# Graph layers on one core: the edge gathers read 128 table rows each instead of 125

## The chip, the cores and the metric

One Trainium2 chip; the program runs on one of its cores. The metric is the time of the whole program on the device, in microseconds (us), lower being better. The engines are named as the profile names them: PE (TensorE, PEld its weight loads), DVE (VectorE), ACT (ScalarE), POOL (GpSimd) and SP (SyncE). SP issues the plain transfers here, POOL the gathers.

## The reference: what is computed

`x` holds 3125 nodes of 256 features; `src` and `dst` are the ends of 50000 edges, ordered by `dst`. Two graph blocks follow each other, each with attention over the nodes and a mixture of experts beside or behind it. What matters here are three passes over all edges:

```python
# two GATv2 layers (one head), each:
xj = (x @ Wl)[src]
h = leaky_relu(xj + (x @ Wr)[dst] + eattr @ We, 0.2)
logits = h @ att
ex = exp(logits - segment_max(logits, dst)[dst])
out = segment_sum(xj * ex[:, None], dst) / segment_sum(ex, dst)[:, None]
...
# later one attention layer with 8 heads of 32 features:
e = leaky_relu(eh[src] + ee + et[dst], 0.2)
ex = exp(e - segment_max(e, dst)[dst])
rst = segment_sum(ft[src] * ex[:, :, None], dst) / segment_sum(ex, dst)
```

In each pass every edge needs the row of its source node from a table in DRAM: a gather of 50000 rows, of 261, 258 and 272 float32 values (1044, 1032 and 1088 bytes) in the three passes.

## The kernel before

**Tiles.** The 3125 nodes are 25 tiles of 125, the 50000 edges 400 tiles of 125. An edge tile that touches two node tiles is worked once for each, so that a pass has S = 432 steps (some of them padding), in NG = 27 groups of G = 16. One step takes one gather of 125 rows, one row to each partition. `schedule` makes the table of row numbers, `c.src_s`, one column for each step.

**One pass** is the function `messages`; it runs three times (stage names `msg1`, `msg2`, `msg3`; the first two with `one` true, the third with eight heads). The profile shows all three under the same names `msg_rows`, `msg_cur` and so on. All engines walk the same groups, each in an instruction stream of its own with a loop over three groups, and meet at semaphores:

- DVE copies the 16 columns of row numbers of a group to `msg_cur` (L142).
- POOL issues 16 gathers a group at L705, into one of RB = 3 buffers of `msg_rows`. Four gathers are a block with a semaphore of its own (`landed[q][b]`). POOL may only start on a block when the sums that read the buffer's last content are done (`summed`).
- SP loads for each group a broadcast of node numbers (`msg_oht`, 875 KB and 101.6 KB) and the masks `msg_pens`.
- PE, for group j+1, multiplies one-hot rows with the destination table (L912; L922 in the third pass) and adds the gathered rows (L916, only in the first two passes), and waits at steps 0, 4, 8 and 12 of a group for the block to land. Between these it sums group j-1 over its edges (L958). At L929 it transposes the logits of group j, once a group: the starts of L929 count the groups off.
- DVE does max, product and sum for the logits (L750, L758, L759), the running maxima, and adds the sums of PE to the totals (L840). In the third pass it also scales the gathered rows (L821) and reads them for the logits (L767), for which it waits for all four blocks.
- ACT scales the gathered rows in the first two passes (L1021) and makes the one-hot matrices.

Before its first group DVE clears the totals (L873) and, in the first two passes, works out the edge terms (L877, L878).

Of the kernel before, what the change touches and what calls it, by code (L numbers as in the profile page):

```python
# [14 lines left out]
I32 = mybir.dt.int32  # L15
# [4 lines left out]
N, D, E = 3125, 256, 50000  # L20
P = 125
EVEN = 112
NT = N // P
ET = E // P
ER = 100
EB = ET // ER
G = 16
S = 432
NG = S // G
RB = 3  # L30
# [4 lines left out]
U = 5  # L35
CN = NT // U

# [157 lines left out]
def transpose_tiles(nc, name, c, src, dst_t, gcol=None, bcol=None, rep=None):  # L195
# [3 lines left out]
    with Stage(nc, name, rep) as st:  # L199
        pt = [[st.ps(f"pt{j}_{k}", [128, P]) for k in range(bufs)] for j in range(2)]  # L200
        turned = st.sem("turned", NT)
        out = [st.sem(f"out{j}", NT) for j in range(2)]
        with st.block() as block:
            @block.tensor
            def _(pe):
                for t in range(NT):
                    if t >= bufs:

                        for j in range(2):
                            pe.wait_ge(out[j].sem, out[j].at(t - bufs + 1))  # L210
                    for j in range(2):
                        last = nc.tensor.transpose(pt[j][t % bufs], src[:, t, j * 128:(j + 1) * 128], c.ident[0:P, 0:P])
                    last.then_inc(turned.sem, 1)

            @block.scalar
            def _(act):
                for t in range(NT):
                    act.wait_ge(turned.sem, turned.at(t + 1))
# [7 lines left out]
            def _(dve):  # L226
                for t in range(NT):
                    dve.wait_ge(turned.sem, turned.at(t + 1))
# [43 lines left out]
def schedule(nc, c, src, dst, ea2, pick, pen):  # L272
# [3 lines left out]
    with Stage(nc, "sch") as st:  # L276
# [28 lines left out]
        sp_ = [st.ps(f"sp{j}", [P, S]) for j in range(6)]  # L305
# [8 lines left out]
        with st.block() as block:  # L314
# [19 lines left out]
            def _(dve):  # L334
                ch = Chain(dve, order)
# [43 lines left out]
                ch(nc.vector.tensor_copy(c.nt_row[:], ntf[0:1, :]))  # L379

                ch(nc.vector.memset(c.src_s[:], 0))
                ch(nc.vector.tensor_copy(c.src_s[:, 0:S], sp_[1][:]))
                ch(nc.vector.memset(c.rel[:], 0.0))
                ch(nc.vector.memset(c.eas[:], 0.0))
                ch(nc.vector.tensor_copy(dsts[:], sp_[2][:]))
# [227 lines left out]
def messages(nc, name, call, c, table, heads, dst_rows, edge_lin, att, acc, marks, ee):  # L613
# [6 lines left out]
    TW = table.shape[1]  # L620
# [3 lines left out]
    PAIRS = G // 2  # L624
    QS = G // 4
    with Stage(nc, name) as st:
        rows = st.sb("rows", [P, RB, G, TW])
        cur = st.sb("cur", [P, RB, G], I32)
        oh = st.sb("oh", [P, RB, G, P])
        oht = st.sb("oht", [K1, RB, G * P])  # L630
        pens = st.sb("pens", [R, RB, 4, P])
# [61 lines left out]
        with st.block() as block:  # L693
            @block.gpsimd
            def _(pool):
                def gather(g, u, i, first):
                    q = u % RB
                    pool.wait_ge(slot_ready.sem, slot_ready.at(g + 1))
                    pool.sem_inc(issued.sem, 1)
                    for b in range(4):  # L700
                        if not first:
                            pool.wait_ge(summed.sem, summed.at((g - RB) * G + (b + 1) * QS))
                            pool.sem_inc(issued.sem, 1)
                        for k in range(b * QS, (b + 1) * QS):
                            nc.gpsimd.indirect_dma_start(out=rows[:, q, k, :], out_offset=None, in_=table,  # L705
                                                         in_offset=bass.IndirectOffsetOnAxis(ap=cur[:, q, k:k + 1], axis=0)).then_inc(landed[q][b].sem, 16)

                for g in range(RB):
                    gather(g, g, 0, True)
                with pool.Fori(0, NG // RB - 1) as i:  # L710
                    for u in range(RB, 2 * RB):
                        gather(i * RB + u, u, i, False)
# [331 lines left out]
def even_parts(ap):  # L1044


    return [(0, EVEN), (EVEN, P)] if ap.shape[0] == P else [(0, ap.shape[0])]

# [1943 lines left out]
def program(nc, I, out):  # L2992
# [12 lines left out]
    c = Consts()  # L3005
    with Stage(nc, "c") as st:
# [1 line left out]
        c.ones_row, c.blocks, c.part = st.sb("ones_row", [1, 512]), st.sb("blocks", [128, 128]), st.sb("part", [128, 1])  # L3008
        c.lin = st.sb("lin", [P, NT])
        c.iota_low = st.sb("iota_low", [P, 16])  # L3010
        c.nt_row, c.src_s = st.sb("nt_row", [1, S], I32), st.sb("src_s", [P, S + G], I32)
        c.rel, c.last, c.eas = st.sb("rel", [P, S]), st.sb("last", [P, S]), st.sb("eas", [P, S, 2])
        c.link, c.gl, c.gf, c.gb = st.sb("link", [1, S + 1]), st.sb("gl", [1, S + 1]), st.sb("gf", [1, NG, G + 1]), st.sb("gb", [1, NG, G + 1])
        c.pen_d, c.rel_d, c.ea_d = scratch("pen_d", [S, 4 * P]), scratch("rel_d", [NG, G * P]), scratch("ea_d", [2, NG, G * P])
# [20 lines left out]
        with Stage(nc, "mx") as s1:  # L3035
            m = s1.sb("m", [P, NT, D])
            norm_table(nc, "nt", c, I, m, c.lin, xn_d, tabs_d[0], xr_d)
            q = s1.sb("q", [P, NT, D])
# [44 lines left out]
        with Stage(nc, "m0") as s1:  # L3083
            gate = s1.sb("gate", [P, 2, NT])
            src_row, dst_row, expert_row = s1.sb("src_row", [P, tiles0], I32), s1.sb("dst_row", [P, tiles0], I32), s1.sb("expert_row", [1, tiles0], I32)
            rows = s1.sb("mv", [P, NT, 2]), s1.sb("rstd", [P, NT]), s1.sb("off", [P, NT])
# [37 lines left out]
            with Stage(nc, "ma") as s2:  # L3124
# [4 lines left out]
                q, k, v = (s2.sb(n, [P, NT, D]) for n in "qkv")  # L3129
# [17 lines left out]
        with Stage(nc, "m1") as s1:  # L3147
            gate = s1.sb("gate", [P, 1, NT])
            src_row, dst_row, expert_row = s1.sb("src_row", [P, tiles1], I32), s1.sb("dst_row", [P, tiles1], I32), s1.sb("expert_row", [1, tiles1], I32)
            rows = s1.sb("mv", [P, NT, 2]), s1.sb("rstd", [P, NT]), s1.sb("off", [P, NT])  # L3150
# [36 lines left out]
```

## Time and profile before

| | |
|---|---|
| time, median of 3 runs | 5575.98 us (5551.09 to 5578.87) |
| the profiled execution, its own time | 5525.67 us |
| its span, first to last instruction | 5523.5 us |
| granted TensorE clock, mean over the span | 0.838 |
| PE busy | 4451.3 us (81%) |
| DVE busy | 2840.2 us (51%) |
| POOL busy | 1959.6 us (35%), of which the 1296 gathers of the passes 1654.3 us |

The gathers of the passes run from 1737.2 us to 4748.3 us of the span, in three stretches. Shares of the whole span say little about a pass, which has limits of its own; a pass is read from its own stretch: 1737 to about 2430 us, 2660 to about 3355 us, 4034 to about 4770 us. An "idle before" of an engine with "issue" behind it is time in which nothing that the profile shows was waited for.

### The profile page before, as it was taken

The page shows a single profiled execution, that of the slowest core. Times are in us where ns is not written, and L with a number is a line of the kernel's source. Part 1 is how long each engine was busy: PE and PEld are TensorE (multiplying, and loading weights), DVE is VectorE, ACT ScalarE, POOL GpSimd, SP SyncE. Part 2 cuts the span into 40 slices and gives each one's busy share as a digit, 9 for nine tenths or more (in the row PEclk, how much of TensorE's full clock was granted, in tenths as well). Part 3 has the DMA queues.
Part 4 walks back from the last instruction along what each step waited for, and adds up shares of the span by engine and source line. Part 5 has one row for each costly group of instructions (what it writes and reads, how often), then busy time and mean ns, then how long its engine had stood idle before and what let it go on. Part 6 is the DMA issues. An engine that isn't in the chain of part 4 may idle for free. (4 is left out here: it accounts for less than half of the span.)

```text
span 5523.5 us, 80735 instructions
## 1 busy us (share of the span) xinstructions
PE 4451.3 (81%) x21805; PEld 3611.6 (65%) x21806; DVE 2840.2 (51%) x8512; ACT 2155.2 (39%) x6526; POOL 1959.6 (35%) x1535
## 2 busy tenths in 40 slices
PE   4649999999995999997789998479468888655694
PEld 2237978888794777765577775379356666445694
DVE  3127263452722666654466664553646666628424
ACT  0124443434442666652366663313333333221222
POOL 0000000000003778840687882046268777300141
PEclk8879999999997999987899997679665555677697
DMA  3340000000004555530555554442565555210613
GB/s 76 82 137 10 1 17 10 17 9 3 16 15 103 124 128 124 128 87 10 119 124 121 128 122 86 140 133 69 123 147 133 128 125 126 66 44 15 210 36 84
DMA packets 423900, 465.87 MB, mean 84 GB/s; under 512 B 223748, under 2 KB 360950, under 8 KB 423111
## 3 DMA queue, kind: packets, MB, share of 16 engines
q1 hardware_dynamic: 228634, 263.29, 18.9%
q0 software_dynamic: 190976, 197.68, 16.2%
q8 instruction: 114, 1.87, 0.1%
q10 hardware_dynamic: 4000, 1.60, 0.1%
q14 instruction: 176, 1.43, 0.1%
HBM read 398.30 MB, written 62.47 MB: 83 GB/s over the span
## 5 line engine op out<-in xcount | busy, mean ns | idle before, releaser
L705 POOL DMA_INDIRECT msg_rows<-tab_d,msg_cur x1296 | 1654.3, 1276 | 1799.0 <-DVE msg_cur L142 1379.7
L958 PE MATMUL msg_agp<-msg_rows,msg_oh 125*125 125x261 f32 (+2 forms) x2592 | 884.4, 471 | 36.1 <-DVE gv_acc L840 27.0
L958 PEld LDWEIGHTS msg_agp<-msg_rows,msg_oh 125*125 125x125 f32 x2592 | 561.2, 229 | 158.9 <-issue 39.7
L912 PE MATMUL msg_zp<-g_xr,msg_oht 127*125 x1728 | 552.7, 402 | 61.7 <-DVE msg_oht L745 61.3
L916 PE MATMUL msg_zp<-msg_rows,c_ident 125*125 125x256 f32 x1728 | 530.8, 388 | 39.8 <-DMA msg_rows<-tab_d,msg_cur 39.7
L1010 ACT ACTIVATE msg_dist<-c_iota,c_rel 125x125 f32<-125x125 f32 x1296 | 492.8, 386 | 46.5 <-PEq L2983 31.6
L750 DVE SCALAR_TENSOR_TENSOR msg_hid<-msg_zp,g_att 125x256 f32<-125x256 f32 x864 | 360.1, 419 | 279.1 <-PE msg_zp L916 266.7
L1014 ACT ACTIVATE msg_oh<-msg_dist,c_ones 125x125 f32<-125x125 f32 x1296 | 492.7, 386 | 0.0
L1000 ACT ACTIVATE msg_ex<-msg_arg 125x16 f32<-125x16 f32 (+1 forms) x81 | 20.0, 247 | 1019.5 <-DVE msg_delta L814 1019.5
L916 PEld LDWEIGHTS msg_zp<-msg_rows,c_ident 125*125 125x125 f32 x1728 | 331.9, 193 | 100.9 <-DMA msg_rows<-tab_d,msg_cur 46.1
L840 DVE TENSOR_TENSOR gv_acc<-gv_acc,msg_agp 125x261 f32 (+1 forms) x864 | 364.1, 421 | 63.2 <-PE msg_agp L958 54.6
L912 PEld LDWEIGHTS msg_zp<-g_xr,msg_oht 127*125 127x125 f32 x1728 | 310.6, 192 | 116.6 <-issue 62.7
L1281 PE MATMUL mix_pb<-mix_ht,mix_w 128*128 128x125 f32 x3200 | 373.5, 275 | 0.0
L1290 PE MATMUL mix_pc<-mix_w,mix_ut 128*125 128x256 f32 x1600 | 361.8, 380 | 7.1 <-ACT mix_ut L1422 7.1
L1281 PEld LDWEIGHTS mix_pb<-mix_ht,mix_w 128*128 128x128 f32 x3200 | 365.6, 192 | 0.4
L1021 ACT ACTIVATE msg_rows<-msg_rows,msg_ex 125x257 f32<-125x257 f32 x864 | 354.3, 497 | 1.7
L1290 PEld LDWEIGHTS mix_pc<-mix_w,mix_ut 128*125 128x125 f32 x1600 | 292.9, 188 | 47.9 <-issue 8.3
L1557 DVE TENSOR_TENSOR mix_t<-mix_pc,mix_b 125x256 f32<-125x256 f32 x100 | 42.5, 425 | 543.5 <-PE mix_pc L1290 543.5
L1243 PE MATMUL mix_pb<-mix_wp,mix_ht 128*125 128x256 f32 x1200 | 282.7, 387 | 4.1 <-ACT mix_ht L1362 4.1
L840 DVE TENSOR_TENSOR ga_acc<-ga_acc,msg_agp 125x264 f32 x432 | 184.4, 427 | 181.4 <-PE msg_agp L958 157.3
L1243 PEld LDWEIGHTS mix_pb<-mix_wp,mix_ht 128*125 128x125 f32 x1200 | 222.6, 192 | 36.4 <-issue 5.5
L1422 ACT ACTIVATE mix_ut<-mix_pb,mix_b 128x125 f32<-128x125 f32 x800 | 215.4, 391 | 30.9 <-PE mix_pb L1281 30.8
(545 smaller groups left out, 7122.0 us busy)
## 6 DMA issues: line engine op xcount, KB each, us to landing
msg_oht<-rel_d SPq DMA_DIRECT2D x81, 875.0 KB
msg_rows<-tab_d,msg_cur POOLq DMA_INDIRECT x1296, 3.9
ee_raw<-in_edge_attr SPq DMA_DIRECT2D x50, 224.0 KB
msg_pens<-pen_d SPq DMA_DIRECT2D x270, 31.2 KB, 8.0
msg_oht<-rel_d SPq DMA_DIRECT2D x81, 101.6 KB
mix_w<-in_L_mix_W SPq DMA_DIRECT2D x8, 1024.0 KB
m0w_wr<-in_L_ffn_w SPq DMA_DIRECT2D x16, 512.0 KB
m0w_w2r<-in_L_ffn_w SPq DMA_DIRECT2D x16, 512.0 KB
```

Of the source, the lines that this page charges most:

```text
L705: nc.gpsimd.indirect_dma_start(out=rows[:, q, k, :], out_offset=None, in_=table, in_offset=bass.IndirectOffsetOnAxis(ap=cur[:, q, k:k + 1] ...
L750: last = nc.vector.scalar_tensor_tensor(out=hid[:, k, :], in0=zp[:, pair_bank(u, k // 2), (k % 2) * D:(k % 2 + 1) * D], scalar=0.0, in1=at ...
L840: nc.vector.tensor_tensor(a_t, a_t, agp[:, sum_bank(u, k), 0:AW], ALU.add).then_inc(combined.sem, 1)
L912: nc.tensor.matmul(z, hots, d_t, start=True, stop=False)
L916: last = nc.tensor.matmul(z, c.ident[0:P, 0:P], rows[:, u % RB, k, 0:D], start=False, stop=True)
L958: nc.tensor.matmul(agp[:, sum_bank(u, k), 0:AW], oh[:, u % RB, k, :], rows[:, u % RB, k, 0:AW], start=True, stop=True).then_inc(summed.sem, 1)
L1010: nc.scalar.activation(dist[:, k % 4, :], c.iota[0:P, 0:P], ACT.Abs, scale=-1.0, bias=c.rel[:, bass.ds(g * G + k, 1)]).then_inc(dist_ready ...
L1014: last = nc.scalar.activation(oh[:, u % RB, k - 1, :], dist[:, (k - 1) % 4, :], ACT.Relu, scale=-1.0, bias=c.ones[0:P, 0:1])
L1021: nc.scalar.activation(r, r, ACT.Copy, scale=ex[:, u % RB, k:k + 1]).then_inc(scaled.sem, 1)
L1243: last = nc.tensor.matmul(pb[bank][0:P, lo:lo + D], ht[:, t % HR, kc, :], wp[:, w, kc, :], start=(kc == 0), stop=(kc == 1))
L1281: last = nc.tensor.matmul(out, w1[:, kc, f * 128:(f + 1) * 128], ht[:, t % HR, kc, :], start=(kc == 0), stop=(kc == 1))
L1290: last = nc.tensor.matmul(pc[t % 2][0:P, 0:D], ut[:, t % 2, f, :], w2[:, f, :], start=(f == 0), stop=(f == FC - 1))
```

## The change

Each gather of a pass now takes 128 row numbers and fills 128 partitions of `msg_rows`. The three added partitions of the table of row numbers stay zero, so that they fetch row 0; nothing reads them. All other instructions see the first 125 partitions as before, but for the copy to `msg_cur`, which is 128 partitions high. The number of gathers, their order and their waits are the same, and so are the instructions of the other engines. The gathers of the two expert stages (98 there and 98 back) stay at 125 rows.

```diff
+ROWS = 128
...
                 ch(nc.vector.memset(c.src_s[:], 0))
-                ch(nc.vector.tensor_copy(c.src_s[:, 0:S], sp_[1][:]))
+                ch(nc.vector.tensor_copy(c.src_s[0:P, 0:S], sp_[1][:]))
...
-        rows = st.sb("rows", [P, RB, G, TW])
-        cur = st.sb("cur", [P, RB, G], I32)
+        rows_all = st.sb("rows", [ROWS, RB, G, TW])
+        rows = rows_all[0:P]
+        cur = st.sb("cur", [ROWS, RB, G], I32)
...
-                            nc.gpsimd.indirect_dma_start(out=rows[:, q, k, :], out_offset=None, in_=table,
+                            nc.gpsimd.indirect_dma_start(out=rows_all[:, q, k, :], out_offset=None, in_=table,
                                                          in_offset=bass.IndirectOffsetOnAxis(ap=cur[:, q, k:k + 1], axis=0)).then_inc(landed[q][b].sem, 16)
...
-        c.nt_row, c.src_s = st.sb("nt_row", [1, S], I32), st.sb("src_s", [P, S + G], I32)
+        c.nt_row, c.src_s = st.sb("nt_row", [1, S], I32), st.sb("src_s", [ROWS, S + G], I32)
```

## Rows read from the trace of the kernel before

**Rows 1.** The page: busy time of the engines

```profile
PE 4451.3 (81%) x21805; PEld 3611.6 (65%) x21806; DVE 2840.2 (51%) x8512; ACT 2155.2 (39%) x6526; POOL 1959.6 (35%) x1535
```

**Rows 2.** Busy time by stretch, first and third pass

```profile
core 0: us, PE busy (x) PEld busy (x) DVE busy (x) ACT busy (x) POOL busy (x), PEclk, DMA share, GB/s
...
1780.00:2440.00 660.00, 606.07 (x2809) 483.31 (x2807) 442.65 (x1890) 419.48 (x1308) 510.79 (x405) 0.98 0.53 120
...
4040.00:4800.00 760.00, 636.35 (x2079) 477.20 (x2079) 501.42 (x1243) 258.60 (x895) 559.62 (x428) 0.58 0.54 121
```

**Rows 3.** The line of the gathers, L705: duration, and issue to landing

```profile
L705 POOL DMA_INDIRECT msg_rows<-tab_d,msg_cur x1296: 1207/1214/2295, 1737.2 to 4748.3; - x186
...
DMA to landing us min/median/max: 3.8/3.9/13.5
```

**Rows 4.** DMA of the stretch 1800 to 2400 us

```profile
DMA packets 53214, 74.77 MB, mean 125 GB/s; under 512 B 36524, under 2 KB 38799, under 8 KB 53164
...
q0 software_dynamic: 48794, 50.22, 38.8%
q1 hardware_dynamic: 4370, 24.11, 16.1%
...
msg_rows<-tab_d,msg_cur POOLq DMA_INDIRECT x382, 3.9
```

**Rows 5.** POOL in order of time, first pass, group 11 (start, duration, idle before)

```profile
2013.28 1.21 POOL L705 DMA_INDIRECT msg_rows<-tab_d,msg_cur  x1 [0.30 <-issue]
...
2017.83 1.21 POOL L705 DMA_INDIRECT msg_rows<-tab_d,msg_cur  x1 [0.30 <-issue]
...
2020.87 1.94 POOL L705 DMA_INDIRECT msg_rows<-tab_d,msg_cur  x1 [0.30 <-issue]
```

**Rows 6.** Waits of the first pass, 1780 to 2440 us (total, times, longest)

```profile
POOL msg_rows L705 <- PE msg_agp L958: 10.4, 27, 1.1
...
PE msg_zp L916 <- DMA msg_rows<-tab_d,msg_cur: 6.3, 3, 4.3
```

**Rows 7.** PE in order of time, first pass

```profile
1757.17 1.22 PE L916 MATMUL msg_zp<-msg_rows,c_ident 125*125 125x256 f32 x2 [11.67 <-DMA msg_rows<-tab_d,msg_cur]
...
1775.10 0.27 PE L929 MATMUL msg_m<-c_ident,msg_lg 125*16 125x125 f32 x1
...
1930.86 0.27 PE L929 MATMUL msg_m<-c_ident,msg_lg 125*16 125x125 f32 x1
...
2027.35 1.04 PE L958 MATMUL msg_agp<-msg_rows,msg_oh 125*125 125x261 f32 x4
2028.24 0.60 PE L912 MATMUL msg_zp<-g_xr,msg_oht 127*125 x2
...
2405.80 0.27 PE L929 MATMUL msg_m<-c_ident,msg_lg 125*16 125x125 f32 x1
```

**Rows 8.** PE in order of time, second pass

```profile
2697.13 0.27 PE L929 MATMUL msg_m<-c_ident,msg_lg 125*16 125x125 f32 x1
...
2829.69 0.27 PE L929 MATMUL msg_m<-c_ident,msg_lg 125*16 125x125 f32 x1
...
3330.82 0.27 PE L929 MATMUL msg_m<-c_ident,msg_lg 125*16 125x125 f32 x1
```

**Rows 9.** DVE in order of time: start of first pass, a loop's turn, third pass

```profile
1758.32 0.73 DVE L878 SCALAR_TENSOR_TENSOR msg_lin_e<-c_eas,g_edge_lin,msg_lin_e 125x432 f32<-125x432 f32 x1
...
2033.48 0.36 DVE L831 TENSOR_SCALAR gv_acc<-gv_acc,msg_fac  x1 [3.79 <-issue]
...
4065.61 0.37 DVE L767 TENSOR_TENSOR msg_lg<-msg_zp,msg_rows 125x128 f32<-125x128 f32 x1 [8.34 <-DMA msg_rows<-tab_d,msg_cur]
...
4088.83 0.37 DVE L767 TENSOR_TENSOR msg_lg<-msg_zp,msg_rows 125x128 f32<-125x128 f32 x1 [7.48 <-DMA msg_rows<-tab_d,msg_cur]
```

**Rows 10.** PE in order of time, third pass, groups 6 and 25

```profile
4225.61 0.30 PE L929 MATMUL msg_m<-c_ident,msg_lg 125*128 125x125 f32 x1 [1.76 <-DVE msg_lg L770]
...
4743.71 0.44 PE L929 MATMUL msg_m<-c_ident,msg_lg 125*128 125x125 f32 x1 [3.06 <-DVE msg_lg L770]
```

## The prediction

> **What bounds the kernel now.** I read the page first, then the busy times by stretch, then the three passes in order of time, engine by engine. PE has the most busy time and POOL only 35% [rows 1], which would make a change to a POOL instruction look idle. But POOL works almost only in the passes. In the stretch of the first pass it is busy 510.79 of 660 us [rows 2], and between two gathers lie 0.30 us in which nothing shown is waited for [rows 5]. A gather takes 1.21 us in the median [rows 3], so one comes every 1.52 us, 16 of them every 24.3 us; one gather of each group is longer by 0.73 us (1.94 against 1.21, [rows 5]), at the time at which DVE compares the 125x2000 node numbers. That makes 25.0 us a group with no gap to spare. The 10.4 us that POOL spent in front of sums of PE are 27 gaps [rows 6], 0.39 us in the mean: hardly more than the usual 0.30. So POOL never stops in the first two passes.
>
> Does anybody wait for it? PE goes through 19 groups of the first pass in 2405.80 - 1930.86 = 474.94 us, 25.0 us each [rows 7], and through 20 of the second in 501.13 us, 25.06 us each [rows 8]. Same pace, which looks like coupling, but is not: within 1780 to 2440 us PE waited for landed rows 3 times, 6.3 us [rows 6]. At group 11 the first block's last gather starts at 2017.83 us [rows 5] and lands about 3.9 us later [rows 3], at 2021.7; PE comes to this group's first step at 2028.24 us [rows 7]. There are 6.5 us of slack. In steady state the pace of PE and DVE sets the first two passes, with POOL just as fast by accident. In the third pass a group takes (4743.71 - 4225.61) / 19 = 27.3 us [rows 10], longer than the gathers need; PE and DVE bound it at a granted clock of 0.58 [rows 2].
>
> What does depend on gathers is the start of each pass, where PE and DVE are hungry: 11.67 us [rows 7] and, in the third, 8.34 and 7.48 us [rows 9], and the first groups of the first two passes.
>
> **The change part by part.** *Instructions.* None is added or moved. The copy of row numbers is three partitions higher: nothing, since work is spread over partitions. Bytes: 3 of 125 rows more, 2.4% of queue 0, which has 38.8% of the DMA engines' time [rows 4]: at most 1 percentage point, hidden while the landed rows have 6.5 us of slack.
>
> *The price of a gather on POOL.* No row shows a gather of another height, so it is bounded. Above: all of the 1.214 us goes with the rows, 1.214 x 128 / 125 = 1.243 us. Below: from the packets. In 1800 to 2400 us, 382 gathers made 48794 packets on queue 0 [rows 4], 128 a gather. 36524 packets of all queues are under 512 B, about 96 a gather, too small for a row of 1044 B. Only some 32 to 35 packets can carry the 125 rows, near four to a packet. The rest is filler, and 128 is 8 for each of 16 engines: it looks as if a gather gave all 16 engines equal lists while rows go to a few of them. If 128 rows spread evenly, 32 packets of four and 16 closing ones do, 48 in place of 128, and if POOL's time goes with packets it is 1.214 x 48 / 128 = 0.46 us. The middle of 0.46 and 1.243 is 0.85; I take 0.95 us, nearer the row measured, since part of it must be fixed. Then a gather comes every 1.25 us, 0.27 us sooner.
>
> The Trainium skill, DMA: Bandwidth & Descriptors, on why a DMA increments its semaphore by 16, says that a transfer runs on the largest number of engines up to 16 that divides its slowest dimension: 5 for 125 rows, 16 for 128. The packet counts agree: 25 rows on each of 5 engines are six packets of four and one of one, with a closing one 8 per engine. By that rule, with POOL's time in proportion to an engine's list (8 rows for 25), a gather would cost 0.39 us and the third pass would get back all 15.8 us below, 6.2 us more than in my sum. The trace cannot show it, as all gathers in it have 125 rows.
>
> *What the faster gather gives back.* First pass: from the first to the seventh L929 155.76 us [rows 7]. Six groups at the steady 25.0 us are 150.0, and the first of them has no sums to do: 16 sums at 0.22 us (four from 2027.35 to 2028.24, [rows 7]), 3.5 us less. So 146.5, a gain of 9.3 us. Second pass: five groups 132.56 us [rows 8] against 5 x 25.06 - 3.5 = 121.8, 10.8 us. The supply follows: by the end of group 1 it is 32 x 0.27 = 8.6 us ahead, and 4.3 us more with each group. The first wait, 11.67 us, can hardly shrink: DVE is busy with its clearing and edge terms until 1758.32 + 0.73 = 1759.05 us [rows 9], and PE gets only three pairs ahead of it. I give 1 us each for the first two passes. Third pass: DVE waits for the whole of group 0, then of group 1; the 32nd gather comes 8.6 us sooner, and I add 1 us for a landing over 16 engines in place of a few: 9.6 of the 15.8 us [rows 9]. Behind these starts nothing is gained: PE and DVE then set the pace, and POOL waits for buffers, late on nobody's path.
>
> Sum: 9.3 + 10.8 + 2 + 9.6 = 31.7 us; I take 30, as some of it meets the next wait. Against the profiled execution that is 5525.67 - 30 = 5496; the three runs have a median 50 us above it, so 5575.98 - 30 = **5546 us**.
>
> **The rivals.**
> - *The gather costs the same or goes with its rows (1.21 to 1.243 us).* Then 16 x 0.029 = 0.46 us a group. Starts: 32 gathers x 0.029 = 1 us each, 3 us. Later 27 x 0.46 = 12.5 us a pass against 6.5 us of slack, 6 us in each of the first two. Together 0 to +15: 5576 to 5591. For it: POOL must read and turn each row number in any case.
> - *POOL gets faster, but the starts are held by something else.* The node numbers, 3 x 875 KB at each start, keep the first rows back; one landing took 13.5 us [rows 3]. Then only the third pass and part of the others come back, 5 to 15 us: 5561 to 5571.
> - *Slower: filling 16 real lists costs POOL more than a few lists and filler.* Its place is L705; its price d each, 16 d a group. Since POOL has no gap in the first two passes, the time is 2 x (432 d - 6.5) + 3 x 32 d. That passes 28 us (0.5%) at d = 0.043, a gather of 1.26 us; with 1.32 us it is +88: 5664 at most. Against it: the filler is made today, too.
> - *More gain than the starts.* DVE loses 3.79 us at a turn of its loop over three groups, in which it waits for nothing shown [rows 9], and PE with it; shorter queues on the DMA engines could shorten this. With 1 to 2 us of it at 8 turns in 3 passes, 24 to 48 us more: 5500 to 5520.
>
> The Trainium skill, SBUF — State Buffer, on who interferes with whom, says that some DVE copies lock POOL out while it writes descriptors. The 1.94 us gather agrees, and that stretch stays under either theory.
>
> **How the numbers follow.** Forecast, 18 to 40 us less: 0.50. Held starts: 0.20. Same or in proportion: 0.15. Slower than 1.26 us a gather: 0.08. More gain: 0.07. A measurement tells about 0.5%, 28 us. Of the forecast two thirds lie beyond it, and all of the last case: faster 0.41; slower 0.08; within it 0.51. The range leaves out the dearer half of the slower cases and the far end of the gain: 5515 to 5583. The forecast's own is 5536 to 5558.
>
> **What the profile will show.** The median of L705 below 1.1 us, if I am right, and above 1.2 in the rival; queue 0 with some 48 packets a gather; the landing below 3.5 us. POOL idle in the first two passes in front of L958, far above 10.4 us. The first six L929 intervals of the first pass near 147 us; the waits of L767 at 0 to 3 us each. The steady groups stay at 25.0 and 27.3 us: if they move by more than 0.3 us, my reading that PE and DVE set their own pace is wrong. If L705 is dearer than 1.26 us, the sign is.

## The result: 4.4% slower, where 0.5% faster was forecast

The changed kernel took 5814.79 us in the median of six runs (5794.38 to 5852.58), the kernel before 5575.08 us (5551.09 to 5590.33) on the same chip: ratio 1.0441, interval 1.0397 to 1.0485. The profiled execution of the changed kernel took 5804.31 us, with a span of 5802.4 us. At the end of this study, on the fifth of the chips that the experiments name (the record doesn't name the one of this result), the same two kernels stood at 0.9907 (0.9872 to 0.9942). Both results are told here.

The price of a gather came out as predicted. The page and the row of the gather's line, after the change (minimum, median and maximum in ns, then the first and the last start):

```profile
PE 4545.9 (78%) x21805; PEld 3648.1 (63%) x21806; DVE 2838.2 (49%) x8512; ACT 2162.2 (37%) x6526; POOL 1621.3 (28%) x1535
```

```profile
L707 POOL DMA_INDIRECT msg_rows<-tab_d,msg_cur x1296: 940/947/6766, 1732.1 to 5020.0; - x186
```

0.947 us against 1.214 [rows 3]; POOL is busy 1621.3 us, 28% of the span, where [rows 1] has 1959.6. The packets fit too. The DMA view of 1800 to 2400 us (queue 0 and its issues), the stretch of [rows 4], shows that 308 gathers made 14774 packets on queue 0, 48 each:

```profile
q0 software_dynamic: 14774, 41.18, 27.5%
...
msg_rows<-tab_d,msg_cur POOLq DMA_INDIRECT x308
```

But the groups of the passes, forecast to stay at 25.0 us, take longer. PE transposes the logits (L929, now L931) once a group. Its row for pass 1 (27 groups), and two neighbours of it from the timeline:

```profile
L931 PE MATMUL msg_m<-c_ident,msg_lg x27: 267/268/415, 1804.2 to 2569.6; 125*16 125x125 f32 x27
```

```profile
1969.95 0.27 PE L931 MATMUL msg_m<-c_ident,msg_lg 125*16 125x125 f32 x1
...
2000.69 0.27 PE L931 MATMUL msg_m<-c_ident,msg_lg 125*16 125x125 f32 x1
```

(2569.6 - 1804.2) / 26 = 29.4 us in the mean, 30.7 between these two, against 25.0 in [rows 7]. The start of the pass, where the gain was forecast, is slower as well: from the first gather to the first L931 it is 1804.2 - 1732.1 = 72.1 us, where it was 1775.1 - 1737.2 = 37.9. From a pass's first gather to its last L931 the three passes take 837.5, 808.2 and 757.3 us, where they took 691.2, 693.8 and 734.2: 284 us more together, and the span grew by 278.9. So the passes hold all of it. What ended the idle time before DVE's first relu step (L750, now L752), in the whole span:

```profile
L752 DVE SCALAR_TENSOR_TENSOR msg_hid<-msg_zp,g_att 125x256 f32<-125x256 f32 x864 | 359.8, 420 | 491.2 <-PE msg_zp L918 240.4 <-remote 196.4 <-issue 45.6
```

A new releaser stands there: "remote", 196.4 us, the profile's word for a signal for which it finds no instruction that had just ended. The same group in the kernel before:

```profile
L750 DVE SCALAR_TENSOR_TENSOR msg_hid<-msg_zp,g_att 125x256 f32<-125x256 f32 x864 | 360.1, 419 | 279.1 <-PE msg_zp L916 266.7
```

One such wait in steady state, on DVE, then PE and POOL at the same time:

```profile
1969.81 0.36 DVE L833 TENSOR_SCALAR gv_acc<-gv_acc,msg_fac  x1 [0.76 <-issue]
1974.58 0.42 DVE L752 SCALAR_TENSOR_TENSOR msg_hid<-msg_zp,g_att 125x256 f32<-125x256 f32 x1 [4.41 <-remote]
```

```profile
1968.64 0.59 PE L918 MATMUL msg_zp<-msg_rows,c_ident 125*125 125x256 f32 x2
...
1971.80 0.60 PE L960 MATMUL msg_agp<-msg_rows,msg_oh 125*125 125x261 f32 x2
1975.50 0.94 PE L960 MATMUL msg_agp<-msg_rows,msg_oh 125*125 125x261 f32 x2 [3.10 <-DVE gv_acc L842]
```

```profile
1968.76 0.94 POOL L707 DMA_INDIRECT msg_rows<-tab_d,msg_cur  x1 [1.01 <-PE msg_agp L960]
1970.00 0.97 POOL L707 DMA_INDIRECT msg_rows<-tab_d,msg_cur  x1 [0.30 <-issue]
1971.28 0.95 POOL L707 DMA_INDIRECT msg_rows<-tab_d,msg_cur  x1 [0.30 <-issue]
1972.54 0.95 POOL L707 DMA_INDIRECT msg_rows<-tab_d,msg_cur  x1 [0.30 <-issue]
1977.23 0.94 POOL L707 DMA_INDIRECT msg_rows<-tab_d,msg_cur  x1 [3.75 <-PE msg_agp L960]
```

The sum that DVE needs ends on PE at 1969.23 us (L918). Its semaphore is recorded as raised only at 1974.56; the five updates of the matmuls that ended behind it, from 1969.67 to 1972.40, follow within 0.25 us, and DVE starts at 1974.58. Meanwhile updates of ACT and DVE are recorded within 0.02 us of the ends of their instructions (DVE's at 1970.18, ACT's at 1970.45, 1971.03, 1972.18 and 1973.34), though about half of ACT's have no record. So it is PE's that are late, not all. PE, whose next sums need DVE, stands 3.10 us; POOL, whose buffers PE frees, 3.75 us. All three engines wait in a ring for a signal whose matmul had ended, after eight gathers nearly without a gap. The 196 us aren't the whole of the 284. With DVE's other groups its remote waits come to 231 us, with POOL's to 252. PE falls idle and loses clock as well; the stretch of [rows 2] in pass 1 is granted 0.89 in place of what stands there, and PE is busy 554 us of 660:

```profile
1780.00:2440.00 660.00, 554.32 (x2350) 429.50 (x2351) 370.57 (x1590) 343.76 (x1059) 331.97 (x339) 0.89 0.40 104
```
At the pass's start, with 48 such gathers in a row, single waits reach 20.9 us.

Two things could be to blame by these rows: what a gather does, and how closely gathers follow each other. The experiments take these apart.

### The profile page after: what moved, and what is told of

The parts are those of the page before. It is cut to its first block and busy times, and to the rows that moved or that the text cites. A ratio compares the mean times of both kernels' runs of the same rounds, so it can differ in the third digit from the quotient of the medians.

```text
span 5802.4 us, 80735 instructions
## 1 busy us (share of the span) xinstructions
PE 4545.9 (78%) x21805; PEld 3648.1 (63%) x21806; DVE 2838.2 (49%) x8512; ACT 2162.2 (37%) x6526; POOL 1621.3 (28%) x1535
## 5 line engine op out<-in xcount | busy, mean ns | idle before, releaser
L707 POOL DMA_INDIRECT msg_rows<-tab_d,msg_cur x1296 | 1317.0, 1016 | 2395.8 <-DVE msg_cur L143 1379.6
L960 PE MATMUL msg_agp<-msg_rows,msg_oh 125*125 125x261 f32 (+2 forms) x2592 | 913.9, 481 | 135.3 <-DVE gv_acc L842 102.5
L914 PE MATMUL msg_zp<-g_xr,msg_oht 127*125 x1728 | 585.8, 422 | 130.0 <-DVE msg_oht L747 61.5
L752 DVE SCALAR_TENSOR_TENSOR msg_hid<-msg_zp,g_att 125x256 f32<-125x256 f32 x864 | 359.8, 420 | 491.2 <-PE msg_zp L918 240.4
L918 PE MATMUL msg_zp<-msg_rows,c_ident 125*125 125x256 f32 x1728 | 558.7, 406 | 12.7 <-DMA msg_rows<-tab_d,msg_cur 12.6
L914 PEld LDWEIGHTS msg_zp<-g_xr,msg_oht 127*125 127x125 f32 x1728 | 325.3, 202 | 195.6 <-issue 138.5
L918 PEld LDWEIGHTS msg_zp<-msg_rows,c_ident 125*125 125x125 f32 x1728 | 350.6, 203 | 78.0 <-DMA msg_rows<-tab_d,msg_cur 14.1
```

The source lines that it names most:

```text
L707: nc.gpsimd.indirect_dma_start(out=rows_all[:, q, k, :], out_offset=None, in_=table, in_offset=bass.IndirectOffsetOnAxis(ap=cur[:, q, k:k ...
L752: last = nc.vector.scalar_tensor_tensor(out=hid[:, k, :], in0=zp[:, pair_bank(u, k // 2), (k % 2) * D:(k % 2 + 1) * D], scalar=0.0, in1=at ...
L914: nc.tensor.matmul(z, hots, d_t, start=True, stop=False)
L918: last = nc.tensor.matmul(z, c.ident[0:P, 0:P], rows[:, u % RB, k, 0:D], start=False, stop=True)
L960: nc.tensor.matmul(agp[:, sum_bank(u, k), 0:AW], oh[:, u % RB, k, :], rows[:, u % RB, k, 0:AW], start=True, stop=True).then_inc(summed.sem, 1)
```

## The experiments

They ran in five groups, each group on one chip beside the kernel before; the results name five chips. The kernel before was profiled on the chip of the result and on the fifth alone: whether it has late signals on the other four isn't known, and each ratio there is taken against its time on that chip. The theories are those of the expectations: A, the gathers' density (their pitch, from start to start); B, their spread over 16 DMA engines, whatever the pitch; C, a bad phase of slots and stages; D, the added row or partitions.

**First chip (kernel before 5592.91 us).** Six register additions ahead of each gather:

```
+                            for _ in range(PAUSE):   # 6
+                                pool.reg_add(spare, spare, 1)
                             nc.gpsimd.indirect_dma_start(...)
```

> Changed kernel (128 rows in a gather), with six register additions on GpSimd ahead of each gather, so that the gathers' starts come further apart than 1.25 us; nothing else is altered. Theory A (density): TensorE's semaphore updates are held up because 16 completion increments per gather at a pitch of 1.25 us leave the path no room; with the pitch back at 1.5 us or more, the group interval goes back from 30.7 to 25.0 us, the held updates are gone and the time is about 5575 us. Theory B (spread): what holds them is that all 16 DMA engines carry rows and report at one moment, whatever the pitch; the interval stays at 30.7 us and the time at about 5815 us. If the additions are hidden and the pitch stays at 1.25 us, both say 5815 us and the run tells nothing.

5825.99 us, ratio 1.042 (1.032 to 1.053), but the pitch stayed at 1.25 us: the additions vanish beside the gather that runs. It tells nothing between A and B, only that a pause must be work of the engine itself.

Then every gather waits for the sum that frees its own buffer, instead of four waiting for the fourth:

```
-                        if not first:
-                            pool.wait_ge(summed.sem, summed.at((g - RB) * G + (b + 1) * QS))
-                            pool.sem_inc(issued.sem, 1)
                         for k in range(b * QS, (b + 1) * QS):
+                            if not first:
+                                pool.wait_ge(summed.sem, summed.at((g - RB) * G + k + 1))
+                                pool.sem_inc(issued.sem, 1)
```

> Changed kernel, in which every gather waits for the one aggregation matmul that frees its own slot, where now four gathers wait together for the fourth; so in steady state the gathers come one by one instead of eight nearly without a gap. The first three groups of a pass still come at 1.25 us. Theory A (density): no hold in steady state, groups back at 25.0 us in passes 1 and 2, the starts still late by 20 to 30 us in each pass: about 5630 us. Theory B (spread): each gather still holds the updates up by itself, 30 us a group and about 5815 us. Rival C (the order of slots and stages has merely locked into a bad phase because GpSimd now catches up): also about 5630 us, but without late updates in the fillings of the pipeline either.

5718.47 us, 1.023 (1.020 to 1.026): in between. PE frees buffers in twos and fours, so the gathers still came in runs at 1.25 us, and the first relu still waited 136 us for remote releases (196 in the changed kernel). Less bunching, less harm: for A, weakly. C isn't borne out, since waits for late signals remained.

112 and 124 rows, to change what a gather carries. These two kernels leave out the rows of 13 edges and of one edge of each step and compute something else; only their times are used:

```
+GR = 112   # or 124
-nc.gpsimd.indirect_dma_start(out=rows_all[:, q, k, :], ..., ap=cur[:, q, k:k + 1]
+nc.gpsimd.indirect_dma_start(out=rows_all[0:GR, q, k, :], ..., ap=cur[0:GR, q, k:k + 1]
+nc.gpsimd.memset(rows_all[:], 0.0)   # once a pass
```

> Each gather fetches 112 rows, none of them the added row 0 (13 of the 125 edges' rows are left out and are zero, blanked once a pass, which may add up to some 20 us a pass at its start by the 1.6 ns per element of the one memset of 128x128). 112 rows divide by 16 as 128 do. Theories A and B: 16 DMA engines, 16 increments, a pitch near 1.25 us: the group interval stays near 30.7 us (5800 us and more). Rival D (the three gathered copies of row 0, or partitions 125 to 127, are what disturbs): the interval goes back to 25.0 us or less, about 5550 to 5600 us with the blanking.

> Each gather fetches 124 rows (one edge's row in 125 is left out, blanked once a pass as in the kernel with 112 rows). 124 divides by 4 and not by 16. If the number of DMA engines that carry rows follows the divisor, four engines carry 31 rows each: the gather costs GpSimd 1.2 us or more, lands later than the 3.8 us of 125 rows on five engines, and there are no late updates of TensorE: groups of 25.0 us by A and B, total 5575 us plus the blanking (0 to 60 us). If the gather is as cheap as with 128 rows (0.95 us), the price doesn't follow the divisor, and A says a group interval near 30.7 us, B 25.0 us.

```profile
L709 POOL DMA_INDIRECT msg_rows<-tab_d,msg_cur x1296: 930/937/2006, 1768.3 to 5006.6; - x186
```

```profile
L709 POOL DMA_INDIRECT msg_rows<-tab_d,msg_cur x1296: 1287/1292/7157, 1752.3 to 4854.1; - x186
```

112 rows (first fence): 0.937 us a gather, pitch 1.24, ratio 1.039 (1.031 to 1.047), remote waits 183 us. No row 0 was added and partitions 125 to 127 weren't touched: D falls. 124 rows (second fence): 1.292 us, pitch 1.60, ratio 1.006 (1.003 to 1.010), no remote waits of that group. A and B both allow it; 124 rows cost more than 125 (1.214 us) and 112 about as much as 128, so the price doesn't go with the row count. What it goes with is worked out further down.

**Second chip (5644.07 us).** A memset of PAD elements ahead of each gather, ordered by a semaphore of its own:

```
+                            pool.wait_ge(padded.sem, padded.at(g * G + k))
+                            apart(pool, padded)
+                            nc.gpsimd.memset(c.ones_row[0:1, 0:PAD], 1.0).then_inc(padded.sem, 1)
                             nc.gpsimd.indirect_dma_start(...)
```

> Changed kernel with a GpSimd memset of one element ahead of each gather, so that the gathers' pitch grows by work of the engine itself (the additions of the first run were hidden behind the gathers: pitch 1.25 us as before). By the 99 to 116 ns of small memsets, with or without another 0.30 us of issue, the pitch should be 1.35 to 1.7 us. Theory A (density): the interval of the groups and the late updates fall with the pitch; at 1.5 us or more the groups are back at 25.0 us and the time is about 5580 to 5600 us, at 1.35 us it lies between. Theory B (spread over 16 DMA engines): nothing changes, groups near 30.7 us, 5815 us or more.

> As the run before, with a memset of 80 elements (estimate 0.24 us at 1.7 ns an element from the memsets of 25 and 200 elements): pitch 1.5 to 1.8 us. Theory A: no late updates, groups of 25.0 us if the pitch is under 1.56 us, else 16 pitches a group (up to 29 us at 1.8 us), with TensorE's updates in time all the same. Theory B: updates as late as in the changed kernel, groups of 30 us or more, and in the third pass too.

The memset went into the 0.30 us between gathers. Pitch 1.25 and 1.27 us, ratios 1.042 (1.037 to 1.047) and 1.040 (1.035 to 1.045): as slow as with no memset, and no test of A yet. They gave the sizes for the third chip.

Every other gather with 128 rows, and all with 126:

```
-out=rows_all[:, q, k, :], ..., ap=cur[:, q, k:k + 1]
+out=(rows_all if k % 2 else rows)[:, q, k, :], ..., ap=cur[0:ROWS if k % 2 else P, q, k:k + 1]
```

> Every other gather reads 128 rows, the others 125; mean pitch (1.25 + 1.52)/2 = 1.38 us. Theory A (density): where between 1.25 and 1.52 us the path gets room isn't known; if at 1.38 us it has enough, groups are back at 25.0 us and the time is about 5560 us, less than both kernels; else slower than 5575 and far less than 5815 us. Theory B: each of the 128-row gathers still holds updates up by itself, half as many: near the middle, 5695 us.

> Each gather reads 126 rows (one added), which divide by 14: if the DMA engines that carry rows follow the divisor, 14 engines carry 9 rows each. Price per gather estimated between the 0.947 us of 128 rows and the 1.214 us of 125, near 0.98 us, pitch 1.28 us. Theory A: slightly less dense than 128 rows: slow, 5750 to 5815 us. Theory B: nearly as many engines report at once: 5780 to 5815 us. If 126 rows cost 1.2 us and keep the time at 5575 us, the divisor isn't what sets the price.

Alternate: 5755.30 us, 1.019 (1.014 to 1.023), near the middle as B says, but A allows it. 126 rows: 0.997 us a gather, pitch 1.30, 1.035 (1.030 to 1.040). The slowdown falls as the pitch grows.

**Third chip (5589.19 us).** The deciding ones: the same memset, long enough to move the pitch, with all gathers at 128 rows.

> As the run with 80 elements, where the memset (0.15 us) went into the 0.30 us between two gathers and the pitch stayed at 1.26 us. By those two runs (0.09 us for 1 element, 0.15 us for 80, 0.16 us between memset and gather) 250 elements take 0.28 us and the pitch is 1.39 us. Theory A (density): late updates clearly fewer, group interval between 25.0 and 30.7 us, ratio to the kernel before 1.00 to 1.03. Theory B (spread): late updates as before, interval near 30.7 us, ratio 1.04.

> 420 elements take 0.41 us and bring the pitch to 1.52 us, that of the kernel before, with 128 rows in each gather. Theory A: updates in time, group interval 25.0 us in pass 1, ratio 1.00. Theory B: late updates as in the changed kernel, interval 30 us or more, ratio 1.04 or more.

> 512 elements take 0.48 us: pitch 1.59 us, that of the 124-row gathers, which ran at 26.3 us a group with TensorE's updates in time. Theory A: as there, 25.5 to 26.3 us a group, ratio 1.005 to 1.01. Theory B: interval of 30 us or more, ratio 1.04 or more.

POOL's timeline with 250 elements, and with 420:

```profile
2001.51 0.95 POOL L712 DMA_INDIRECT msg_rows<-tab_d,msg_cur  x1 [0.16 <-issue]
2002.46 0.30 POOL L711 MEMSET c_ones_row<- 1x250 f32 x1
2002.91 0.95 POOL L712 DMA_INDIRECT msg_rows<-tab_d,msg_cur  x1 [0.16 <-issue]
```

```profile
2001.44 0.95 POOL L712 DMA_INDIRECT msg_rows<-tab_d,msg_cur  x1 [0.16 <-POOL c_ones_row L711]
2002.39 0.44 POOL L711 MEMSET c_ones_row<- 1x420 f32 x1
2002.99 0.95 POOL L712 DMA_INDIRECT msg_rows<-tab_d,msg_cur  x1 [0.16 <-POOL c_ones_row L711]
```

The relu step in these two:

```profile
L758 DVE SCALAR_TENSOR_TENSOR msg_hid<-msg_zp,g_att 125x256 f32<-125x256 f32 x864 | 360.0, 420 | 393.4 <-PE msg_zp L924 267.6 <-remote 66.6 <-issue 49.5
```

```profile
L758 DVE SCALAR_TENSOR_TENSOR msg_hid<-msg_zp,g_att 125x256 f32<-125x256 f32 x864 | 360.1, 420 | 301.3 <-PE msg_zp L924 253.2 <-issue 25.6 <-remote 10.1
```

Pitch 1.41 us: 1.028 (1.025 to 1.031), remote waits 67 us. Pitch 1.55: 5557.20 us, 0.995 (0.993 to 0.997), remote waits 10 us. Pitch 1.62: 1.009 (1.006 to 1.011), no remote waits of that group; there 16 x 1.62 = 25.9 us bound the group. B falls: 128 rows on 16 DMA engines do no harm once the pace is that of the kernel before. Where the faster gather lost time, it lost it by following more closely on the one before.

128 rows only where PE has nothing to do yet:

```
+                            n = ROWS if first and g == 0 else P
```

> 128 rows only in the 16 gathers of each pass's first group, 125 in all others. While they are issued TensorE has nothing to do in the pass, so under A and B no update of it can be held up; the first group lands 15 x 0.267 = 4 us earlier in each of the three passes: 12 us less than before, 5563 against 5575 us (ratio 0.998), if the first group's rows are what the start waits for. If even these gathers disturb, the ratio is above 1.

5604.70 us, 1.003 (1.001 to 1.005). I had expected 0.998; remote waits of 57 us appeared, though only the first 16 gathers of a pass ran at 1.25 us. The 125-row gathers behind them took 1.18 to 1.20 us here, not 1.21, for a reason that I can't name; their pitch was 1.49 to 1.51. Either such a small step is enough, or what the dense start piles up lasts. This run doesn't tell which.

**Fourth chip (5647.04 us).** Where it begins, the 420 elements again, and the kernel before's 125-row gathers with the one-element memset as a control.

> 128 rows with a memset of 300 elements: by the measured pitches (1.411 us with 250 elements, 1.548 us with 420) 0.81 ns an element, pitch 1.45 us. Theory A, with the turning point between 1.41 and 1.52 us: if it lies at the top of this stretch, as the 125-row gathers at 1.49 to 1.51 us in the run with 16 dense gathers first hint, late updates remain and the ratio is 1.015 to 1.025; if the effect falls evenly from 1.41 to 1.55 us, 1.015. Theory B, which the runs at 1.55 and 1.62 us speak against: 1.04.

> As before with 360 elements: pitch 1.50 us. If the disturbance ends only above 1.51 us, DVE still waits some 50 us for updates recorded late in all and the ratio is 1.003 to 1.012; if it ends by 1.48 us, the ratio is 0.993 to 0.997, since the pitch is shorter than with 420 elements.

> The 420-element kernel again, with more rounds: is it really faster than the kernel before, whose pitch (1.52 us) is shorter than its 1.55 us? Theory A gives it nothing over the kernel before, ratio 1.000 to 1.005 by the 0.03 us x 16 that a group of gathers is longer; the first measurement was 0.995 [0.993, 0.997]. If that stands, 128 rows spread over 16 DMA engines are worth something by themselves once the pace is held.

> Control: the gathers of the kernel before (125 rows), with the one-element memset, its semaphore and its wait ahead of each. The memset goes into the 0.30 us between gathers, so the pitch should stay at 1.52 us and the ratio at 1.00. If the filling itself disturbed, as the late updates in the kernels with it might be read, late updates appear here too and the ratio is above 1.01.

Pitch 1.45: 1.012 (1.007 to 1.018). Pitch 1.50: 1.016 (1.011 to 1.020). Pitch 1.55: 1.005 (1.003 to 1.007). The runs at 1.45 and 1.50 can't be told apart. The 0.995 of the third chip didn't come again. The control, at 1.53 us: 1.004 (1.002 to 1.006), with 60 us of remote waits, against none in the profile of the kernel before at 1.52. Between those two stands one thing besides the chip: the memset raises its own semaphore, and `apart` another, so that 18 updates come with a gather instead of 16.

**Fifth chip (5542.43 us).** The kernel before and the changed one, as they are.

> The kernel before itself, profiled once more, on a chip of this series of runs. In its first profile no update of TensorE is late and the 864 relu steps of DVE wait 279 us, none of it put down to a remote release. If its pitch of 1.52 us leaves the path room on any chip, that is so again, and the lateness in the control with 125 rows and a memset (60 us) comes from the memset. If the kernel before sits just at the edge, as the control and the two runs with 420 elements (10 and 32 us) hint, its profile now shows 20 to 60 us of such waits and groups of 26 to 27.5 us instead of 25.1 us. Ratio 1.00 either way.

> The changed kernel itself on the same chip: ratio 1.03 to 1.045, relu steps of DVE with some 200 us of remote waits, groups of 28 to 31 us; if the kernel before is at the edge and slower on this chip, the ratio lies at the lower end.

The expectation of the second was wrong, and this is the surprise of the study: 5492.79 us, ratio 0.9907 (0.9872 to 0.9942), of two executions, where the kernel before, run once more as an experiment, gave 1.0006 (0.9992 to 1.002) to itself. The changed kernel's relu row and POOL's gathers in pass 1 on this chip:

```profile
L752 DVE SCALAR_TENSOR_TENSOR msg_hid<-msg_zp,g_att 125x256 f32<-125x256 f32 x864 | 360.0, 420 | 262.7 <-PE msg_zp L918 250.1
```

```profile
L931 PE MATMUL msg_m<-c_ident,msg_lg x27: 268/268/269, 1768.8 to 2421.2; 125*16 125x125 f32 x27
L707 POOL DMA_INDIRECT msg_rows<-tab_d,msg_cur x432: 940/946/2059, 1735.2 to 2400.7; - x144
```

The kernel before there:

```profile
L929 PE MATMUL msg_m<-c_ident,msg_lg x27: 267/268/269, 1781.0 to 2441.0; 125*16 125x125 f32 x27
L705 POOL DMA_INDIRECT msg_rows<-tab_d,msg_cur x432: 1207/1211/2326, 1743.4 to 2424.4; - x144
```

The gathers' pitch is 1.25 us as before, and no "remote" is left. Groups take (2421.2 - 1768.8) / 26 = 25.1 us. From the first gather to the last turn of the logits a pass takes 686.0, 678.7 and 723.9 us against 697.6, 690.6 and 734.2.

**All of them side by side.** "Updates" is the number of semaphore updates that the trace holds; the memset kernels send 2592 more, the one in which each gather waits some 860 more, the others the same.

| chip | gathers | pitch us | relu's remote waits us | updates in the trace | ratio |
|---|---|---|---|---|---|
| of the result | 125 rows (before) | 1.52 | 0 | 55890 | 1 |
| of the result | 128 rows (changed) | 1.25 | 196 | 35033 | 1.044 |
| first | 128, additions | 1.25 | 181 | 35340 | 1.042 |
| first | 112 | 1.24 | 183 | 35278 | 1.039 |
| first | 128, each waits | in runs of 1.25 | 136 | 38396 | 1.023 |
| first | 124 | 1.60 | 0 | 45789 | 1.006 |
| second | 128, memset 1 | 1.25 | 92 | 35482 | 1.042 |
| second | 128, memset 80 | 1.27 | 95 | 36048 | 1.040 |
| second | 126 | 1.30 | 256 | 36154 | 1.035 |
| second | 128 and 125 | 1.25, 1.52 | 55 | 39423 | 1.019 |
| third | 128, memset 250 | 1.41 | 67 | 40106 | 1.028 |
| third | 128, memset 420 | 1.55 | 10 | 48942 | 0.995 |
| third | 128, memset 512 | 1.62 | 0 | 52358 | 1.009 |
| third | 16 of 128, then 125 | 1.49 to 1.51 | 57 | 41029 | 1.003 |
| fourth | 128, memset 300 | 1.45 | 66 | 39703 | 1.012 |
| fourth | 128, memset 360 | 1.50 | 67 | 41402 | 1.016 |
| fourth | 128, memset 420 | 1.55 | 32 | 46173 | 1.005 |
| fourth | 125, memset 1 | 1.53 | 60 | 43613 | 1.004 |
| fifth | 125 (before) | 1.52 | 0 | 55842 | 1.001 |
| fifth | 128 (changed) | 1.25 | 0 | 55668 | 0.991 |

The column of remote waits has one group only; over all of DVE's groups they come to 276 and 265 us with the memsets of 1 and 80 elements, beside 231 in the changed kernel, so the 92 and 95 aren't a smaller harm.

Within each of the first three chips the harm falls as the gathers move apart. It is within 0.5% by 1.55 us; beyond that, at 1.60 and 1.62 us, POOL's own pace costs 0.6 and 0.9%. And the late signals go with records that are missing: in the three traces that are whole, nothing is late; where 35 to 39% of the updates that a kernel sends are missing, the time is 3.5 to 4.4% longer. Missing records alone don't make a kernel slow: 18% are missing with 124 rows, without a remote wait, and 27% with 16 gathers of 128, at a ratio of 1.003. Of the 20857 that the changed kernel's trace lacks, all but some 730 lie in the three passes: up to the first gather both traces hold 9285 updates, and from there to pass 1's last L931 4932 in place of 11117.

## Why the prediction was wrong

**The price: right.** 0.947 us for an estimate of 0.95, pitch 1.25, 48 packets a gather. With the other row counts the price can now be read. If 126 rows go to 14 engines, 9 each, and 124 to four, 31 each, and all 16 engines get lists as long as these, a gather makes 4 x 16 = 64 and 9 x 16 = 144 packets; queue 0 shows 19076 for 298 gathers, 64.0, and 52506 for 365, 143.9. The prices are 0.947, 0.997, 1.214 and 1.292 us for 48, 64, 128 and 144 packets, about 0.79 us and 3.3 ns a packet (0.79 + 0.0033 x 144 = 1.27). That 0.95, chosen between bounds of 0.46 and 1.243, came so near was luck in part; the form, a fixed part and one by packets, was right, and time in proportion to packets (0.46 us) or to an engine's list (0.39 us) was far off.

**The starts of the passes: wrong on the chip of the result, right where the signals arrive in time.** On the chip of the result the first L931 of passes 1 and 2 comes 34 us later behind the first gather than before, and the first six intervals of pass 1 take 165.8 us for a forecast near 147. On the fifth chip the passes gained 11.6, 11.9 and 10.3 us, for terms of 9.3 + 1, 10.8 + 1 and 9.6: 33.8 us, for a sum of 31.7. The first six intervals of L931 in pass 1 came to 145 us. POOL waited 112 us in front of the sums from 1780 to 2440 us, "far above 10.4", and DVE's two waits for rows in the third pass fell to 2.93 and 5.51 us, forecast at 0 to 3 each. How soon a gather lands the traces of the changed kernel don't show, so the 1 us that the sum gives to that is open. The whole span shrank by 5535.8 - 5476.8 = 59.0 us there. Of the other 25 us, 8.1 lie ahead of the first gather. Some 16 lie in the stage between the first two passes, which runs the same work at a granted clock of 0.82 instead of 0.74; this stage, in the changed kernel and in the kernel before:

```profile
2435.00:2636.00 201.00, 149.83 (x553) 102.17 (x553) 84.10 (x207) 54.28 (x134) 3.03 (x6) 0.82 0.16 40
```

```profile
2455.00:2672.00 217.00, 166.34 (x554) 110.98 (x553) 84.10 (x207) 54.66 (x135) 3.03 (x6) 0.74 0.15 37
```

PE is busy 16.5 us less for 553 and 554 matmul entries, the whole difference of the stretches. I had no term for the clock of a stage that the change doesn't touch. Why it was granted more there isn't shown; one profile of each kernel stands behind it.

**The step that failed** is this: "Behind these starts nothing is gained: PE and DVE then set the pace, and POOL waits for buffers, late on nobody's path." That PE and DVE set the pace holds only while their signals arrive. I took a POOL that gets ahead for harmless, and named the test myself (groups that move by more than 0.3 us). They moved by 4.4 us in the mean of pass 1 on the chip of the result (29.4 against 25.0), where three passes became 284 us longer, and by 0.1 on the fifth. The slower rival had the right sign and another mechanism: a gather dearer than 1.26 us. No rival had the faster gather itself do harm.

**What is shown, and what isn't.** Shown, on the chips where the harm appears: it is the pitch and not the rows, the row count or the 16 engines (420 and 512 elements against 250, on one chip); what DVE waits for is PE's semaphore updates, recorded up to 5 us late in steady state while PE's matmuls had ended. It comes on the chip of the result and on the first four named ones, and not on the fifth, at the same pitch of 1.25 us: the pitch alone isn't the whole condition. Not shown is what holds the signals. DMA packets aren't slower in it: a data packet of 4176 B took 214 ns in the median of pass 1 on the chip of the result and as much on the fifth (162 ns in the kernel before, on both).

What fits best, as I see it, is the recording itself. Every gather ends in 16 updates, 12.8 per us at a pitch of 1.25 us and 10.5 at 1.52. In a whole trace each update leaves a record, the records that are missing go with the delay, and how fast records are carried off may differ from chip to chip; the control fits too, with 18 / 1.53 = 11.8 updates per us and 60 us of remote waits, beside 18 / 1.55 = 11.6 (10 and 32 us) and 18 / 1.62 = 11.1 (none). Other runs don't fit a single limit on that rate: 250 elements make 18 / 1.41 = 12.8, as many as the changed kernel, at a ratio of 1.028 instead of 1.044, and 126 rows 16 / 1.30 = 12.3 at 1.035, where 300 elements make 18 / 1.45 = 12.4 at 1.012. The ratios follow the pitch better than this rate, with chips mixed. The Trainium skill, NOTIFIC — the notification-queue block, section 7.1 on overflow, says that the block which writes such records always holds its producers back in its internal pipeline rather than lose a record inside it, and that a full ring drops new records in one of its modes and stalls the producer in another. Producers held back and records dropped would together give both signs, late updates and missing records; no run here shows that block at work. Every time in this study comes with a span and a clock, so none is known to be free of recording, and no run here tests it. If it is so, the 4.4% would belong to the recorded execution, and the 0.9% gain of the fifth chip would be nearer to what the kernel does by itself. If it is not, the signals themselves are slow at this pace on some chips. That stays open.

## What to carry to other kernels

Padding the row count of a gather to a multiple of 16 made it 22% cheaper for GpSimd here (1.214 to 0.947 us), and where the signals arrived in time, the gain lay where engines wait for first rows, as the waits at the starts of the passes said. Before a faster issuer of DMAs is called free, look at how many semaphore updates per microsecond it can make in a burst, and read in the profile of after whether a consumer waits although its producer had ended ("remote", and updates that are recorded in a bunch). Count the updates in both traces: if many are missing, measure on another chip before the change is judged, even though records can be missing where the time is the same.

## What was not expected of the hardware

- The same pair of kernels stood at 1.0441 (1.0397 to 1.0485) and at 0.9907 (0.9872 to 0.9942) on two chips or at two times; the medians of the kernel before alone ranged from 5542.43 to 5647.04 us over all groups of runs.
- While PE's updates were recorded up to 5 us late, those of ACT and DVE that have a record were on time, within 0.02 us.
- Register additions ahead of a gather are hidden (six of them: pitch 1.25 us), and so, but for 0.02 us, is a memset of up to 80 elements (0.15 us), in the 0.30 us between two gathers. From 80 elements on, 0.16 us lie between a memset and the gather behind it.
- 128 rows are cheaper to gather than 125 or 124: 0.947, 1.214 and 1.292 us.
